# First cross attention: a second score product in place of turned probabilities

## The reference

```
x = x + attention(norm(x))                 # layer 0, 16 heads of 64, causal
x = x + cross_attention(norm(x), context)  # layer 0: the stage that is changed
x = x + mixture_of_experts(norm(x))
x = x + linear attention, cross attention, mixture of experts (layer 1)

def cross_attention(x, z):                 # 16 heads of 16
    Q, K, V = x @ Wq.T, the two halves of z @ Wkv.T
    attn = softmax(Q K^T * 16 ** -0.5)     # 100 x 361 per head and sequence
    return (attn V) @ Wo.T
```

## Time and profile before

| | us |
|---|---|
| median of 3 runs | 3470.06 (3465.08 to 3473.06) |
| the profiled execution, first to last instruction (its span) | 3436.3 |
| TensorE (PE) busy | 3266.1 (95%) |
| its weight loads (PEld) | 2434.1 (71%) |
| VectorE (DVE) busy | 1887.3 (55%) |
| ScalarE (ACT) busy | 1649.4 (48%) |
| GpSimd (POOL) busy | 785.1 (23%) |

### The profile page before, as it was taken

One profiled execution on the slowest core, in us unless ns is written; L12 is line 12 of the kernel. 1 busy time (PEld: TensorE's weight loads), 2 busy tenths in 40 slices (PEclk: granted clock), 3 DMA queues, 4 the chain that ended last, 5 costly groups with the idle time before them and its releaser, 6 DMA issues. The chain is left out here.

```text
span 3436.3 us, 76398 instructions
## 1 busy us (share of the span) xinstructions
PE 3266.1 (95%) x24682; PEld 2434.1 (71%) x24683; DVE 1887.3 (55%) x5145; ACT 1649.4 (48%) x4614; POOL 785.1 (23%) x854
## 2 busy tenths in 40 slices
PE   8999999999999989999998999999999999998992
PEld 6777776666666666677776776777777777766871
DVE  4555555677777755122222664666666666663433
ACT  4555555666666620122222326666666666652220
POOL 1000000000000000333332210132332332336874
PEclk9999999999999999999999999999999999999996
DMA  8600000300000051211112100010000000025784
GB/s 269 171 0 0 0 0 0 144 11 11 9 11 11 5 166 35 82 31 31 30 28 46 51 0 5 18 44 20 18 15 11 14 13 12 13 81 139 203 230 133
DMA packets 136408, 181.30 MB, mean 53 GB/s; under 512 B 36156, under 2 KB 108601, under 8 KB 135308
## 3 DMA queue, kind: packets, MB, share of 16 engines
q1 hardware_dynamic: 84112, 133.96, 12.6%
q0 software_dynamic: 45760, 26.67, 4.8%
q10 hardware_dynamic: 6460, 19.66, 1.5%
HBM read 116.11 MB, written 103.61 MB: 64 GB/s over the span
## 5 line engine op out<-in xcount | busy, mean ns | idle before, releaser
L1279 DVE TENSOR_REDUCE e_nmx<-PS 128x1 f32<-128x361 f32 x416 | 221.5, 533 | 341.6 <-PE PS L1126 335.6
L1654 ACT ACTIVATE b_p<-PS,b_nmx 100x361 f32<-100x361 f32 x512 | 267.6, 569 | 150.2 <-DVE b_nmx L1743 150.2
L901 POOL DMA_INDIRECT slot_rows<-r_row,r_rows_now x256 | 257.3, 1005 | 336.1 <-DVE e_p L1286 289.7
L1126 PE MATMUL PS<-e_cT,e_qT 128*128 128x361 f32 x832 | 333.5, 483 | 0.0
L1231 ACT ACTIVATE e_pT<-PS 121x384 f32<-121x384 f32 (+1 forms) x416 | 199.4, 480 | 220.1 <-PE PS L1133 220.0
L2678 PE MATMUL PS<-c_wgu,c_tile_xT 128*128 x912 | 290.7, 462 | 7.2 <-issue 6.4
L1133 PEld LDWEIGHTS PS<-ident,e_p 128*121 128x121 f32 x1248 | 197.9, 184 | 96.2 <-ACT e_pT L1231 0.4
L1743 DVE TENSOR_REDUCE b_nmx<-PS 100x1 f32<-100x361 f32 x512 | 243.8, 526 | 39.0 <-PE PS L1499 39.0
L1236 ACT ACTIVATE e_p<-PS,e_nmx 128x361 f32<-128x361 f32 x416 | 232.8, 560 | 36.2 <-DVE e_nmx L1279 36.2
L1506 PEld LDWEIGHTS PS<-ident,b_p 100*121 100x121 f32 x1536 | 188.2, 185 | 63.3 <-ACT b_pT L1638 33.3
L1506 PE MATMUL PS<-ident,b_p 100*121 100x100 f32 x1536 | 223.1, 280 | 8.8 <-ACT b_pT L1638 6.7
(11 more groups left out here) (340 smaller groups left out, 6492.4 us busy)
## 6 DMA issues: line engine op xcount, KB each, us to landing
f_w<-in_f_W SPq DMA_DIRECT2D x64, 384.0 KB, 3.8
slot_rows<-a_empty SPq DMA_DIRECT2D x1, 21504.0 KB, 65.3
f_xg<-slot_rows SPq DMA_DIRECT2D x64, 336.0 KB, 4.0
c_wgu<-in_c_GU ACTq DMA_DIRECT2D x8, 1408.0 KB, 12.0
sum<-X SPq DMA_DIRECT2D x2, 3200.0 KB, 57.4
f_sums<-sum SPq DMA_DIRECT2D x16, 400.0 KB
b_cT<-in_ctx_T SPq DMA_DIRECT2D x32, 181.5 KB, 2.3
e_cT<-in_ctx_T SPq DMA_DIRECT2D x32, 181.5 KB
```

The lines of the kernel that those rows point to most:

```text
L901: pool.indirect_dma_start(out=self.rows, in_=self.row[:, u, :], in_offset=None, out_offset=bass.IndirectOffsetOnAxis(ap=self.rows_now[:, u ...
L1126: sr.fill_done(pe.matmul(sr.at(f"s{m}", ROWS, CTX), qT[:, at:at + ROWS], cT[:, u, 0:CTX], start=True, stop=True), f"s{m}")
L1279: dve.tensor_reduce(nmx[:, m:m + 1], sr.at(f"s{m}", ROWS, CTX), AX.X, ALU.max, negate=True).then_inc(max_ready, 1)
L1654: sr.move_done(act.activation(p[:, g % 2, a, 0:CTX], sr.at(f"s{g}{a}", S, CTX), ACT.Exp, bias=nmx[:, g, a:a + 1]), f"s{g}{a}")
```

## The change

The probabilities are no longer turned. In their place the scores are computed a second time, already turned (keys on partitions, queries on columns), and the exponent is taken there and written straight to `pT`. The maximum must then be subtracted ahead of the product: each head's unused 16 rows of its tile serve for this. `kT` is kept twice, once per parity r; row 16 (1 - r) of each tile is set to one by ScalarE's copy (`mark` as bias, `unmarked` as scale), and VectorE's reduces write the negated maxima to column 16 (1 - r) of the head's 32 columns of a cleared `nmx`. One transpose (`w`) turns `nmx`, VectorE adds it to the queries (`qS`), and the second product over 32 rows gives score minus maximum.

- The first product goes six slots ahead, the maxima's turning and the addition five, the second product four, the weighing three.
- Bank plan: both products use three pairs of banks (0 to 5) through the new class `Pairs`, in the order s-half 0, s-half 1, p-half 0, p-half 1 of each slot; a half is two row tiles, one bank each. Pieces, `w` and the sums `o` share a ring of two banks (6, 7), in the order piece, piece, w, o.
- VectorE reduces two banks (2 x 361) at a time; ScalarE takes the exponent of two banks (2 x 300) at a time, without bias, and copies sums once per group instead of once per sequence.
- The order in a slot: TensorE has the two pieces, `w`, first product, second product, weighing; ScalarE its pieces, the exponents, the sums; VectorE its pieces, the addition, the two reduces.
- Pieces are placed two to a slot by a table; the loop body holds two turns, since the queries are double-buffered; the first turn is a partial turn of the same body, and all engines' start waits for the cleared constants.
- SP loads the context of sequence 0 behind v02 and of sequence 1 behind k11 of the turn before, where it was behind v02 and v12.

```diff
+class Pairs(Ring):
+    def __init__(self, k, first, n):
...
+        self.filled = [k.filled[first + 2 * b] for b in range(n)]
+        self.moved = [k.moved[first + 2 * b] for b in range(n)]
+    def plan(self, names):
+        self.bank = {name: n % self.n for n, name in enumerate(names)}
+        self.order = {name: n // self.n for n, name in enumerate(names)}
...
+    def one(self, name, half, p, n):
+        return self.PS[0:p, self.first + 2 * self.bank[name] + half, 0:n]
+    def both(self, name, p, n):
+        at = self.first + 2 * self.bank[name]
+        return self.PS[0:p, at:at + 2, 0:n]
...
-    AHEAD, TURNED, WEIGHED = 4, 3, 2
+    LAST_KEYS = CTX - (CH - 1) * KEYS
+    SCORED, SHIFTED, TURNED, WEIGHED = 6, 5, 4, 3
+    PIECES = [("xT", "k00"), ("q", "k01"), ("r0", "k10"), ("t0", "v00"), ("y0", "v02"), ("r1", "v10"), ("t1", "v12"),
+              ("k11", "y1")]
...
-        sr = Banks(k, 0, 4).plan([f"s{g}{a}" for g in range(GROUPS) for a in range(TILES_R)])
-        tr = Banks(k, 4, 2).plan([f"p{g}{a}" for g in range(GROUPS) for a in range(TILES_R)])
-        ob = Banks(k, 6, 1).plan(["o0", "o1"])
-        mr = Ring(k, 7, 1).plan(["v10", "v12", "xT", "k00", "r0", "t0", "q", "k01", "y0", "v00", "v02", "k10",
-                                 "r1", "k11", "t1", "y1"])
+        sr = Pairs(k, 0, 3).plan([f"{a}{group(n, by)}{half}" for n in range(GROUPS)
+                                  for a, by in (("s", SCORED), ("p", TURNED)) for half in range(2)])
+        names = [m for n in range(GROUPS) for m in (*PIECES[n], f"w{group(n, SHIFTED)}", f"o{group(n, WEIGHED)}")]
+        mr = Ring(k, 6, 2).plan(names)
...
+                    mr.wait_full(sp, "v02", i - 1)
+                    load(0, i + 1)
+                    mr.wait_full(sp, "k11", i - 1)
                     load(1, i + 1)
...
+                pool.memset(nmx[:], 0.0).then_inc(prepared, 1)
...
-                pool.memset(p[:, :, :, CTX:KEYS * CH], 0.0).then_inc(prepared, 1)
...
+                def scores(n, i, par):
...
+                    for half in range(2):
+                        sr.wait_free(pe, f"s{g}{half}", i)
                     for a in range(TILES_R):
                         rows = slice(32 * a, 32 * a + 32)
+                        last = pe.matmul(sr.one(f"s{g}{a // 2}", a % 2, S, CTX),
+                                         qT[rows, buffer(n, SCORED, par), tile, r, u * S:(u + 1) * S],
+                                         kT[rows, u, tile, r, 0:CTX], start=True, stop=True)
+                        if a % 2:
+                            sr.fill_done(last, f"s{g}{a // 2}")
+                def turn_maxima(n, i):
+                    mr.wait_free(pe, f"w{g}", i)
+                    sr.wait_moved(pe, j, f"s{g}0", f"s{g}1")
+                    mr.fill_done(pe.transpose(mr.at(f"w{g}", 128, S), nmx[:, g % PAR].rearrange("p a n -> p (a n)"),
+                                              k.ident[0:S, 0:S]), f"w{g}")
+                def turned_scores(n, i):
+                    mr.wait_moved(pe, j, f"w{g}")
+                    for half in range(2):
+                        sr.wait_free(pe, f"p{g}{half}", i)
                     for c in range(CH):
                         for a in range(TILES_R):
+                            rows = slice(32 * a, 32 * a + 32)
+                            last = pe.matmul(sr.one(f"p{g}{a // 2}", a % 2, KEYS, CH * S)[:, c * S:(c + 1) * S],
+                                             kT[rows, u, tile, r, c * KEYS:(c + 1) * KEYS], qS[rows, r, :],
+                                             start=True, stop=True)
...
+                def turn(i, par, this, nxt):
                     for n in range(GROUPS):
+                        for m in PIECES[n]:
+                            if this if m in OWN else nxt:
+                                piece(m, i)
+                        if ahead(n, SHIFTED, this, nxt):
+                            turn_maxima(n, i)
+                        if ahead(n, SCORED, this, nxt):
+                            scores(n, i, par)
+                        if ahead(n, TURNED, this, nxt):
+                            turned_scores(n, i)
+                        if ahead(n, WEIGHED, this, nxt):
+                            weigh(n, i)
...
+                    for r in range(PAR):
+                        last = act.activation(kT[:, u, t, r, :], mr.at(f"k{u}{t}", 128, KEYS * CH), ACT.Identity,
+                                              bias=mark[:, r:r + 1], scale=unmarked[:, r:r + 1])
+                def exponents(n, i):
+                    for half in range(2):
+                        sr.wait_full(act, f"p{g}{half}", i)
+                        sr.move_done(act.activation(pT[:, g % 2, 2 * half:2 * half + 2, :],
+                                                    sr.both(f"p{g}{half}", KEYS, CH * S), ACT.Exp), f"p{g}{half}")
...
+                def maxima(n, half, i):
+                    sr.wait_full(dve, f"s{g}{half}", i)
+                    sr.move_done(dve.tensor_reduce(nmx[:, r, 2 * half:2 * half + 2, 16 * (1 - r)],
+                                                   sr.both(f"s{g}{half}", S, CTX), AX.X, ALU.max, negate=True),
+                                 f"s{g}{half}")
+                def shift(n, i, par):
+                    mr.wait_full(dve, f"w{g}", i)
+                    mr.move_done(dve.tensor_tensor(qS[:, r, :],
+                                                   qT[:, buffer(n, SHIFTED, par), tile, r, u * S:(u + 1) * S],
+                                                   mr.at(f"w{g}", 128, S), ALU.add), f"w{g}")
```

More of the change, by code:

```diff
@@ L198, in pass_over_in, with done @@
             pe.sem_inc(self.moved[self.bank[m]], 1)
+class Pairs(Ring):
+    def __init__(self, k, first, n):
+        self.PS, self.first, self.n, self.uses = k.PS, first, n, k.uses
+        self.filled = [k.filled[first + 2 * b] for b in range(n)]
[3 more added lines that the diff above has]
+        self.order = {name: n // self.n for n, name in enumerate(names)}
+        self.per = [len(range(b, len(names), self.n)) for b in range(self.n)]
+        assert len(self.bank) == len(names)
+        self.base = [self.uses[self.first + 2 * b] for b in range(self.n)]
+        return self
+    def done(self, turns):
+        for b in range(self.n):
+            self.uses[self.first + 2 * b] += turns * self.per[b] + sum(self.bank[n] == b for n in self.own)
+    def one(self, name, half, p, n):
[3 more added lines that the diff above has]
+        return self.PS[0:p, at:at + 2, 0:n]
 def layer_norm(dve, ln, step, t, i, xs, stored=None):
@@ L1496, in scores @@
                     for a in range(TILES_R):
                         rows = slice(32 * a, 32 * a + 32)
[L1498 to L1508, removed]
@@ new lines, in weigh @@
+                def weigh(n, i):
+                    g, (_, j) = group(n, WEIGHED), before(n, i)
+                    u, x = g // G, g % G
+                    mr.wait_free(pe, f"o{g}", i)
+                    if x == 0:
+                        mr.wait_moved(pe, (i, i - 1)[u], f"v{u}2")
+                    sr.wait_moved(pe, j, f"p{g}0", f"p{g}1")
+                    for c in range(CH):
+                        rows = KEYS if c < CH - 1 else LAST_KEYS
+                        for a in range(TILES_R):
@@ new lines, in piece @@
+                def piece(m, i):
+                    if m == "xT":
+                        turn_x(i)
+                    elif m == "q":
+                        queries(i)
+                    elif m[0] == "k":
+                        keys(int(m[1]), int(m[2]), i)
+                    elif m[0] == "v":
+                        values(int(m[1]), int(m[2]), i)
+                    elif m[0] == "r":
+                        turn_sums(int(m[1]), i)
+                    elif m[0] == "t":
+                        turn_out(int(m[1]), i)
+                    else:
+                        out(int(m[1]), i)
@@ L1627, in _ @@
-                with pe.Fori(0, TURNS - 1) as i:
-                    turn(i, True, True)
-                turn(TURNS - 1, True, False)
+                pe.wait_ge(prepared, PREPARED)
+                turn(-1, 1, False, True)
+                with pe.Fori(0, (TURNS - 1) // 2) as m:
+                    for par in range(2):
+                        turn(2 * m + par, par, True, True)
+                turn(TURNS - 2, 0, True, True)
+                turn(TURNS - 1, 1, True, False)
             @block.scalar
@@ new lines, in turn @@
+                def turn(i, par, this, nxt):
+                    for n in range(GROUPS):
+                        for m in PIECES[n]:
+                            if this if m in OWN else nxt:
+                                piece(m, i, par)
+                        if ahead(n, TURNED, this, nxt):
+                            exponents(n, i)
+                        if ahead(n, WEIGHED, this, nxt):
+                            move_sums(n, i)
+                        if not this:
```

(9 more changed lines are left out.)

342 lines of the change are left out of this document (101 added, 241 removed).

## The result

The changed kernel takes 3663 us (median of 4 runs, 3652 to 3681); beside it on the same chip the kernel before takes 3471 us. The ratio is 1.056, with a 95% interval of 1.053 to 1.059: slower by 192 us, where 124 was forecast. The time of 3663 lies in the whole range (3550 to 3670), but 7 us under its upper end, and outside the forecast's own range (3560 to 3635). The wait named first is the largest part of the loss; about a third of the loss has two causes that the sum did not hold.

The account below looks back on a forecast made before the run. TensorE's own work bounds the kernel (36.3 us a turn). After: 30.9 work + 9.2 + 4.9 waits = 45.0; fifteen turns +130, ends -6: 3470 + 124 = 3594 us. Own range 3560 to 3635 (43 to 47 a turn), whole 3550 to 3670.

Parts of the forecast that it names:

- The wait named first: TensorE's second product waits in every slot for VectorE's reduce of the same slot's first product: 9.2 us per turn.
- The wait for the reduce: Bank pair of s0 reused by p1 in the same slot, so TensorE waits for VectorE: 1.13 us per slot.
- The wait for the sums: A slot's second piece needs the bank of the previous slot's sums, which ScalarE copies after both exponents: 4.3 us per turn.
- 1.26 for the exponents: In the wait for the sums, the time of ScalarE's two exponents ahead of its copy: 1.26 us.
- 0.1 back: In the wait for the sums, the handover from ScalarE's copy to TensorE: 0.1 us.
- The maxima's wait for the queries' copies: In the slot of q, the maxima wait until ScalarE has made both copies of the queries: some 0.6 us.
- TensorE's own work: Per turn, 36.3 less 12.6 of turning, plus eight times 0.18 (maxima) and 0.72 (second product): 30.9 us.
- The case of 1.31 us for a product bound by its loads: Rival: weight loads bind the second product, 1.31 us in place of 0.72; 75 us more, 3669; chance 0.10.
- The gain of 12 us from fewer changes of tiling: On TensorE, three tiling changes per slot instead of four, 0.09 us each, 12 us; left out of the sum.
- The ends of the stage: Start before the first whole turn and last turn after the loop: together 6 us less than before.
- I get 32: The start, against 33.8 us before: v's clearing, three slots without waits, four at some 4.5 us.
- The clock: Rival: the new waits lower TensorE's clock once a turn, 16 x 1.7 = 27 us more, 3621; chance 0.09.

Follow-up runs that it names:

- e3: The changed kernel with the reduce of half 0 looking at 120 of the 361 keys; 3545 us, ratio 1.030.
- e7: The changed kernel with TensorE's loop written out, without a backward branch in the stage; 3608 us, ratio 1.048.
- c1: The changed kernel itself, not edited, run again on a second chip; 3632 us against 3441, ratio 1.055.
- e8: The changed kernel with TensorE's loop written out and three idle products in each wait for the reduce; 3595 us against 3472, ratio 1.036.
- e5: The kernel before with only TensorE's loop body in this stage doubled to two turns; 3476 us against 3441, ratio 1.011.
- e6: The changed kernel with the pieces moved between the two score products and TensorE's loop written out; 3417 us against 3441, ratio 0.994.
- e9: e6 without TensorE's wait for the cleared constants, with idle products in the partial turn's first two slots; 3434 us against 3472, ratio 0.989.

## Why the prediction was right or wrong

**The wait for the reduce: right.** From the bank plan it was to be 1.13 us in each of 128 slots. It is 0.99 to 1.10, 131 us in all against the 140 written down, and e3 shows that TensorE waits for that reduce and nothing else. The 0.15 us that I took from VectorE to TensorE was nearer 0.06 (767.05 + 0.91 to 768.02).

**The wait for the sums: right in kind, too large.** I had 4.3 us per turn. The waits of lines 1523, 1529 and 1592 add up to 34 us in 16 turns, 2.1 each (2.5 in a turn at full clock), where 50 to 70 us was to show it. The steps that failed are "1.26 for the exponents" and "0.1 back": in the slot after 768.02 the exponents hold ScalarE for 1.11 and the way back takes 0.06. Besides, a piece with nothing behind it holds TensorE for its whole row (0.39 for t, where I took 0.33), so that the waits come to 0.3 to 0.8 us where I had 0.35 to 1.1:

```profile
768.02 0.89 PE L1567 MATMUL PS<-b_qS,b_kT 32*121 32x100 f32 x24 [1.00 <-DVE b_nmx L1741]
...
768.95 1.23 ACT L1689 ACTIVATE b_pT<-PS 121x600 f32<-121x600 f32 x2 [1.57 <-PE PS L1567]
...
770.06 0.26 ACT L1669 ACTIVATE b_sums<-PS 128x100 f32<-128x100 f32 x1
...
770.38 1.12 PE L1529 MATMUL PS<-b_wv,b_cT 128*121 128x256 f32 x4 [0.49 <-ACT b_sums L1669]
```

The maxima's wait for the queries' copies, "some 0.6", is 0.56.

**TensorE's own work: a little more.** 30.9 us per turn in the sum, 32.6 busy in e7's clean turn. The second product takes 0.83, where I took 0.72 between ends of 0.65 and 1.31; over eight slots that is 0.9 of the 1.7, and where the other 0.8 lies I have not traced. The case of 1.31 us for a product bound by its loads did not come: 24 loads of 121 columns in 0.83 are 0.035 each, where six loads of 121 columns on the full array came every 0.12 (910.45 to 911.16 before), so the loads of the four row tiles overlap. The gain of 12 us from fewer changes of tiling can't be seen apart. Work too low by 1.7 and waits too high by about 2 cancel, so that 45.0 came out near the 44.3 to 44.7 of turns at clock 1.00 (c1, e7). That is luck in part, too.

**The ends of the stage: wrong by some 15 us.** I had start and last turn together 6 us shorter than before. In e8 they are 9 us longer. The stretches of the profiles, in us (the start is from the stage's first idle product to TensorE's first instruction of turn 0):

| | before | forecast | e8 | e7 | c1 |
|---|---|---|---|---|---|
| start | 37.0 | 35.2 | 46.6 | 53.3 | 51.9 |
| fifteen whole turns | 544.4 | 675 | 660.2 | 694.7 | 713.2 |
| last turn | 22.7 | 18 | 21.7 | 22.8 | 19.7 |
| stage | 604.1 | 728 | 728.5 | 770.7 | 784.8 |

The step that failed is "I get 32": the clearing of v delays the start by the 3 us named, but behind it come four gaps of 1.7 to 2.7 us, 8.1 in all in e8. The profile puts them down to TensorE's own queue at line 198 ("PEq L198" above), where the partial turn counts off the uses of banks that it leaves out. I had written these slots down as without waits. And the mean granted clock of the start is 0.78 in e8, 0.60 in e7 and 0.66 in c1, against 0.91 before. In e8 the start takes 11 us more than forecast, the last turn 4 more, and the fifteen turns 15 less.

**The clock: the term that was left out.** I gave it a chance of 0.09 as a case of its own, "once a turn", 27 us, and left it out of the sum. The granted clock over the stage is 0.89 in the first profile and 0.92 in c1. e8 against e7 prices what the waits bring: 1.036 against 1.048, or 42 us of the stage. Some 10 of these are the 0.7 us per turn by which the filled turns are shorter at full clock as well (44.0 against 44.7), for a reason that no run shows; 23 are low stretches in the loop's turns and 7 lie in the start. So the clock proper costs some 30 us, about what the rival said, and the error was to hold it for unlikely and for another case than the forecast: both happened. What misled me is that I judged a single wait of 1.1 us, though it comes back in each of 128 slots.

**The loop's return: not in the prediction at all.** The change's description said that the loop body holds two turns, and I gave this no price. It costs 14 us of the stage (c1 against e7) and 24 in the medians. The stops themselves are 19.9 us, six of them, by the "issue" before line 1505. The Trainium skill (Runtime: NRT & Kernel Launch, Instruction fetch mechanics) has the rule that I should have weighed: a taken branch whose target is not in the two pages held makes the engine wait until that page is loaded. It gives TensorE a store of 2048 instructions, filled in blocks of 256. The trace agrees that a return can stop the engine and that the length of the body decides: with two turns in the body of the kernel before (1622 products and loads, and the waits between them) there are six stops of 2.8 to 3.4 us (e5). It does not bear out the two pages: one turn is 406 products and 405 loads, more than two blocks of 256, and its return shows no stop. Where between one turn and two the limit lies, no run measured.

**The sum for the second chip.** By the stage's length: work and waits 124 us (e8 against before), what the waits bring through the clock and the 10 us named 42 (e7 against e8), the returns 14 (c1 against e7), together 181 of the 191. The other 10 lie behind the stage, where nothing was changed: the profiled runs take 2234 us there in the kernel before, 2235 in e7, 2247 in c1 and 2279 in the first changed one. No cause of the change is known for them. The profiles are of several chips; a turn at full clock is the same on two of them (33.67 us in e6 and in e9).

**The ranges.** By the same sum, the ends of 43 and 47 us per turn give 3565 and 3625, not the 3560 and 3635 written. 3663 is in neither. It is inside the whole range only because that was drawn out for a product bound by its loads (3669), which did not happen.

**The span.** I read 33.8 us between the profiled span and the median as something that lies around the span. It is not: the changed kernel's profiled run has a span of 3679.2 and a time of 3680.9. With the same 1.7 us, the profiled execution of before was one of some 3438 us (an estimate), as this kernel takes on the second and third chip. The difference cancels in a forecast made as a change, and it would not in one made as a time.

## What to carry to other kernels

When a plan of banks names its uses in order, count the uses of a slot modulo the ring: where that puts a product on the bank of the product issued immediately before it, the reader's whole time becomes TensorE's wait, and independent pieces belong between the two and not ahead of both. A wait that recurs in every slot should be priced with the clock that it may cost as well; a copy of the kernel with idle products in the wait reads it off. A loop body that is doubled for the sake of a double buffer should be checked for stops at its return: by "issue" idle time at the body's first instruction, and by the q8 line of the page. And when a forecast meets its number, compare the parts: here errors of 11 and 4 us one way and 15 the other cancelled to 1.

## What the runs showed of the hardware

- Doubling TensorE's loop body from one turn to two, with unchanged work, made it stop for 2.8 to 3.4 us at each of the loop's six returns and raised the packets of instruction loads from 47 to 108. In the changed kernel written out (e7) the stops went, while the packets went only from 117 to 106. So it is the return that costs, not the number of loads.
- In e7, where TensorE is idle for 1.1 us in each slot of 5.6 us and 0.3 to 0.8 more in most, and never for longer at once, the granted clock fell in ten of 14 turns. Filled with idle products to 39.5 us busy of 44.0 (e8), it stayed at 1.00 in all 14. A microsecond at the low level cost 0.45 us.
- The changed kernel varied by 29 us over its first four runs (3652 to 3681) with the mean granted clock at 0.953 to 0.964, the slowest run at the lowest clock.
- A row-tiled product of 32 x 121 by 100 columns on four row tiles, three chunks and two passes, took 0.83 us of TensorE.
